# Four row scatters in flight instead of two in the dispatch stage of a two-layer mixture-of-experts kernel

## The reference

```python
x = x + _L0_attn_ref(_layernorm(x), ...)   # 16 heads of 16, causal
x = x + _L0_ffn_ref(_layernorm(x), ...)    # 16 experts, top 2, one shared expert
x = x + _L1_attn_ref(_layernorm(x), ...)   # 16 query heads, one key and value head
x = x + _L1_ffn_ref(_layernorm(x), ...)    # 32 experts, top 8, one shared expert
```

```python
logits = flat @ router_w.T
_, topk_idx = jax.lax.top_k(logits + router_bias, TOPK)
for e in range(N_EXPERTS):
    h = jax.nn.silu(flat @ Wu[e]) * (flat @ Wg[e])
    out = out + combine[:, e:e + 1] * (h @ Wd[e])
for s in range(N_SHARED):
    out = out + jax.nn.silu(flat @ Su[s]) * (flat @ Sg[s]) @ Sd[s]
```

## Time and profile before

| | us |
|---|---|
| median of 3 runs | 1201.76 |
| lowest and highest run | 1192.37, 1206.13 |
| the profiled execution's own time | 1202.92 |
| its span | 1201.1 |

### The profile page before, as it was taken

How to read it: one execution, slowest core, us unless ns; L and a number is a source line. 1 busy time by engine, 2 the same in 40 slices (tenths; PEclk the granted TensorE clock), 3 DMA queues, 4 the chain that set the end, 5 groups by cost and what they waited for, 6 DMA issues and landing times. The chain is left out here.

```text
span 1201.1 us, 22110 instructions
## 1 busy us (share of the span) xinstructions
PE 909.2 (76%) x5927; PEld 701.8 (58%) x5927; DVE 697.1 (58%) x2692; ACT 462.5 (39%) x1172; POOL 624.3 (52%) x878
## 2 busy tenths in 40 slices
PE   2578888888596995179898888628799999999900
PEld 1466666666354883156676655414488887888800
DVE  4778888863532554557677665523245554555568
ACT  2446566653101441247645444200044444444400
POOL 3546565533063554245638888756245655555610
PEclk9858899897688998558969778658899999999955
DMA  8400000000633542300002222229455555555378
GB/s 233 180 2 1 1 1 2 1 2 1 230 110 108 147 137 91 112 1 2 2 1 84 83 94 100 99 100 404 185 164 166 176 174 157 168 152 166 96 300 330
DMA packets 72791, 136.99 MB, mean 114 GB/s; under 512 B 13102, under 2 KB 51421, under 8 KB 70624
## 3 DMA queue, kind: packets, MB, share of 16 engines
q1 hardware_dynamic: 51840, 85.15, 21.9%
q0 software_dynamic: 17632, 46.73, 10.9%
q10 hardware_dynamic: 3200, 3.70, 0.9%
HBM read 79.15 MB, written 62.39 MB: 118 GB/s over the span
## 5 line engine op out<-in xcount | busy, mean ns | idle before, releaser
L2051 POOL DMA_INDIRECT parts<-e_y,e_dest x206 | 202.6, 984 | 186.1 <-issue 98.1
L1946 PE MATMUL e_ps_u<-wres,e_xT 128*128 x824 | 215.4, 384 | 0.1
L1367 POOL TENSOR_SCALAR_AFFINE_SELECT a_probs<-a_probs 128x256 f32<-128x256 f32 x256 | 108.7, 449 | 134.3 <-ACT a_probs L844 133.4
L1946 PEld LDWEIGHTS e_ps_u<-wres,e_xT 128*128 128x128 f32 x824 | 158.0, 193 | 23.4 <-issue 2.0
L1453 POOL DMA_INDIRECT rows<-f_rows,f_place_at x128 | 124.7, 974 | 51.8 <-issue 27.4
L1959 PE MATMUL e_ps_y<-wres,e_hT 128*128 x412 | 124.8, 385 | 8.5 <-ACT e_hT L1992 5.5
L844 ACT ACTIVATE a_probs<-a_ring 128x768 f32<-128x768 f32 x128 | 104.7, 818 | 67.6 <-PE a_ring L611 66.1
L1987 ACT ACTIVATE e_act_out<-e_ps_u 128x128 f32<-128x128 f32 x206 | 57.1, 277 | 180.7 <-issue 95.6
L2016 DVE TENSOR_TENSOR e_hid<-e_act_out,e_ps_u 128x128 f32<-128x128 f32 x206 | 59.3, 288 | 111.1 <-PE e_ps_h L1954 50.2
L1041 DVE CUSTOM_DVE_ANT_0 a_masked<-a_ring,a_ahead 128x128 f32<-128x128 f32 (+1 forms) x256 | 76.0, 352 | 53.9 <-PE a_ring L587 50.8
L2025 DVE TENSOR_SCALAR e_y<-e_ps_y,e_xg 128x256 f32<-128x256 f32 x206 | 99.5, 483 | 1.0 <-issue 1.0
(11 more groups left out here) (300 smaller groups left out, 2036.3 us busy)
## 6 DMA issues: line engine op xcount, KB each, us to landing
e_xg<-rows SPq DMA_DIRECT2D x159, 160.0 KB
wres<-in_experts SPq DMA_DIRECT2D x4, 3072.0 KB
f_rows<-parts SPq DMA_DIRECT2D x8, 1024.0 KB, 7.1
f_xT<-parts SPq DMA_DIRECT2D x8, 1024.0 KB, 7.5
e_xg<-rows SPq DMA_DIRECT2D x47, 144.0 KB
wres<-in_experts SPq DMA_DIRECT2D x4, 1536.0 KB
rows<-empty SPq DMA_DIRECT2D x1, 5120.0 KB, 24.3
e_yk<-parts SPq DMA_DIRECT2D x16, 256.0 KB
```

Of the source, the lines that this page charges most:

```text
L1367: last = nc.gpsimd.affine_select(out=diagonal[:, :, a], in_=diagonal[:, :, a], compare_op=ALU.is_ge, fill=0.0, base=0, pattern=[[0, 2], [1 ...
L1946: last = nc.tensor.matmul(ps_u[b % 2][:, 0:2 * P], xT[b % 2][:, c * P:(c + 1) * P], wres[:, ds(e, 1), 2 * c * P:2 * (c + 1) * P].rearrange ...
L2051: nc.gpsimd.indirect_dma_start(out=parts[:, :], out_offset=bass.IndirectOffsetOnAxis(ap=dest[b % NY][:], axis=0), in_=y[b % NY][:], in_off ...
```

## The change

In `dispatch` the number of semaphores, and with it the number of scatters that may be on their way, becomes IN_FLIGHT = 4 in place of 2. Scatter n waits for scatter n - 4. At the end POOL waits for each of the four semaphores to have its 8 scatters.

```diff
@@ -1524,7 +1524,7 @@
-        scattered = [sem(f"scattered{i}") for i in range(2)]
+        scattered = [sem(f"scattered{i}") for i in range(IN_FLIGHT)]
@@ -1551,12 +1551,12 @@
             for t in range(NT):
                 for k in range(K):
                     n = t * K + k
-                    wait(pool, scattered[n % 2], 16 * (n // 2))
+                    wait(pool, scattered[n % IN_FLIGHT], 16 * (n // IN_FLIGHT))
                     nc.gpsimd.indirect_dma_start(
                         out=rows[:, :], out_offset=bass.IndirectOffsetOnAxis(ap=place_at[:, t, k:k + 1], axis=0),
-                        in_=X[:, t], in_offset=None).then_inc(scattered[n % 2], 16)
-            for i in range(2):
-                pool.wait_ge(scattered[i], 16 * K * NT // 2)
+                        in_=X[:, t], in_offset=None).then_inc(scattered[n % IN_FLIGHT], 16)
+            for i in range(IN_FLIGHT):
+                pool.wait_ge(scattered[i], 16 * K * NT // IN_FLIGHT)
```

## The result

| | before | after |
|---|---|---|
| median | 1198.85 us (4 runs, 1192.37 to 1206.13) | 1220.03 us (4 runs, 1211.65 to 1223.26) |
| profiled execution, span | 1201.1 | 1217.8 |
| ratio after / before | | 1.0195, 95% interval 1.0155 to 1.0235 |

The change makes the kernel about 2% slower; 1198 us had been forecast, with 1192 to 1204 as the range. The same kernel was timed twice more with experiments: 1220.17 us against 1196.73 (ratio 1.0216, interval 1.0150 to 1.0282) and 1219.07 against 1196.63 (1.0179, interval 1.0124 to 1.0235).

What follows compares the result with a forecast made beforehand. `dispatch` was taken as bound by POOL's scatter chain, last at the closing barrier by 3.7 us over PE and DVE's chain. Sum -3.7 + 0 + 0 = -3.7 us: 1201.76 - 3.7 = 1198.1, rounded 1198 us, range 1192 to 1204.

Steps and rivals of the forecast that it cites:

- POOL's pace: Scatters in `dispatch`: without landing waits, starts 1.26 us apart with 0.30 us gaps, the last ending 4.1 us earlier.
- The tail: End of `dispatch`: last scatter's end to the end of POOL's DRAIN stays 4.46 us, so POOL is through at 374.4.
- Rival (a): POOL's DRAIN in `dispatch`: the tail grows to 8.1 us as in attention; saving 0.5, time 1201.3; chance 0.13.
- rival (b): POOL's DRAIN in `dispatch`: work left undone per scatter adds up to 8.0 us owed; slower, 1205.7; chance 0.06.
- Rival (c): Scatters in `dispatch`: landings or POOL already limit the pace, waits only move to n-4; saving 0, 1201.8; chance 0.09.
- (d): PE's clock at the expert stage's start: 1.0 us lost or 2.2 won, 1199.1 or 1195.9; inside the forecast's range.
- DVE reports at 374.8, untouched by the edit: Barrier ending `dispatch`: DVE's report stays at 374.8 and becomes last, so release moves from 378.5; 3.7 us saved.
- The last part of the prediction: List of signs: wrong if PE's or DVE's chain itself ends later, or layer 1 changes by more than the shift.
- The barrier and what follows: After `dispatch`: POOL's barrier instruction right behind DVE's report; clear, second barrier, SP's load (376.8) and PE's start (379.0) move along.
- The rest of the kernel: Expert stage, reduction and layer 1: the shift passes through unchanged, as nothing there waits for a fixed time.

Runs made afterwards that it cites:

- e10: The changed kernel again, unaltered, as control for three further runs; two times, 1199.86 and 1181.77 us, before 1183.94; `dispatch` 65.0 us.
- e16: Against before: 32 extra four-deep scatters of 64-byte rows ahead of the real ones, plus 1200 semaphore increments by SP in attention 0; 1226.35 us against 1185.62.
- e2: The changed kernel's four semaphores, but scatter n waits for scatter n - 2 as before; 1210.48 us against before's 1216.53, ratio 0.9982.
- e4: The changed kernel, but every eighth scatter waits for the one before it; 1213.37 us against before's 1216.53, ratio 0.9980.
- e1: The changed kernel with three semaphores and three scatters in flight instead of four; 1242.18 us against before's 1216.53, ratio 1.0200.
- e3: The changed kernel with one tiny POOL memset behind every scatter; 1230.28 us against before's 1216.53, ratio 1.0102.
- e9: The changed kernel once more, unaltered, as a control; 1220.17 us against before's 1196.73, ratio 1.0216.
- e17: The changed kernel again, unaltered, timed in five rounds; 1219.07 us against before's 1196.63, ratio 1.0179.
- e14: The kernel before, two in flight, plus 600 semaphore increments issued by SP once the slots are ready; 1184.44 us against 1188.92, ratio 0.9982.
- e6: The changed kernel, but scatter 16 alone waits for scatter 15; 1179.79 us against before's 1184.46, ratio 0.9961.
- e8: The changed kernel, but scatter 8 alone waits for scatter 7; 1184.62 us against before's 1184.46, ratio 0.9979.
- e13: The changed kernel, but scatter 16 alone waits for scatter 15, timed again beside a control; 1184.60 us against before's 1183.94, ratio 1.0008.
- e18: Same kernel as e16 (extra thin scatters, SP increments in attention 0), run again in another series; 1254.60 us against before's 1196.63.

## Why the prediction was wrong

**POOL's pace: right.** Forecast were starts 1.26 us apart with gaps of 0.30 us and 40.3 us from the first start to the last end; measured 1.27 us, 0.30 us, and 372.09 + 0.96 - 332.64 = 40.4 us. The landing was as quick as the step assumed: 2.5 us (median of e10). With the 0.30 us gap this gives (2.5 + 0.3) / 2 = 1.40 us for two in flight, the pace of before. The Trainium skill's page "DMA: Bandwidth & Descriptors", section "Anatomy of one DMA", gives an estimate of 2.34 us for these rows and of 2.0 us for the thin ones; e10 has 2.5 us and e16 2.1 for them. The measured times bear the rule out. What the prediction drew from it, that the change would then save nothing, left out the gap.

**The tail: right.** From the end of the last scatter to the end of the DRAIN 377.5 - 373.1 = 4.4 us, forecast 4.46. Rival (a), 8.1 us, and rival (b), an owed backlog, both fall; (b) had the sign of the result, but by POOL's own arrival, which came 22.4 us before the release. Rival (c) falls too, since no scatter waited. So does (d): the half clock ends at 408.8, 4.6 us behind PE's start at 404.20, against 4.4 in before.

**"DVE reports at 374.8, untouched by the edit": the step that failed.** It reported at 399.9. The prediction had priced what the edit does to POOL and to the barrier and took the other chain as given, because no instruction of it was touched and no engine or port was shared that the profile of before showed. The last part of the prediction named this as what would make it wrong, but no case and no chance stood for it. What the runs showed in its place: in the series with late increments those of PE came up to 15 us late at that addition once POOL no longer waited, and DVE reported 25.1 us later. In before POOL's short waits are spread over the whole run (11.3 us in 24 of them): e2, which has them too, and e4, with three breaks, have no stall; after, e1, e3, e9 and e17, where they are gone, have it. Those waits had been booked as pure loss. No row of before priced this, though its trace already has PE increments 0.7 to 3.6 us late in both expert stages and in attention 1, where POOL issues DMAs too; why the increments are late stays open.

**The barrier and what follows: right.** POOL's barrier instructions follow the last report within 0.1 us (399.9, 400.0), and the next stage starts on PE 4.2 us after the release, 404.20 - 400.0, as in before (382.72 - 378.5). A saving of the forecast size is there where nothing is held back: 65.0 us in e10 against 68.2 in e14, so 3.2. In the first series it is in the sum too, hidden: DVE came 25.1 us later, of which 3.7 fill the time that POOL used to be last, and the stage began 1.5 us later (counted from the clearing of the semaphores, L109, at 310.9 and 312.4), so 25.1 - 3.7 - 1.5 = 19.9 us of stage.

**The rest of the kernel: right.** Attention 1, `finish` and experts 1 together +2.6 - 0.4 - 1.9 = +0.3 us. Nothing was forecast for experts 0 either; its -4.9 us goes with the late increments in the trace of before, told above.

No kernel tried here beats both. Those with breaks are within 0.4% of before (e4 in a series with late increments, ratio 0.9980; e6, e8 and e13 in series without, 0.9961, 0.9979 and 1.0008), and the 3 us that the change brings at best is 0.3%, less than these intervals tell apart.

## What to carry to other kernels

A wait on a queue that issues DMAs back to back is not only lost time: before taking it away, look for a chain on other engines that runs beside it, give "that chain is slowed" a case and a price, and keep a break every few issues if the gain is small anyway. When two engines that wait for different things start in the same instant, with "remote" or "issue" as the releaser and the producers long done, look whether the increments were late and not the work. And when an experiment takes an effect away, run the unchanged kernel in the same series before believing it: eleven of the runs here met a series without the effect.

## What the runs showed of the hardware that had not been expected

- While POOL issues indirect DMAs 1.27 us apart without a break, PE's semaphore increments can come 15 us late (362.30 to 377.69 in after) and 20.0 us in e9, and in e18, with 64 scatters, the additions that wait for them stand up to 32 us apart. They come in order, the last ones 60 ns apart. In after, e1, e9 and e17 the last addition that is held back starts 0.1 to 0.4 us behind the end of POOL's 2.67 us DRAIN, in e3 and e18 before that end. Those of DVE and ACT are not held (0.04 us at most).
- It happened in four series of runs of eight, and there with over 40% of the DMA increments missing from the record, most of all in the stage that stalls. In the other four it never happened, and the kernel before was 8 to 33 us faster (1184 to 1189 us against 1197 to 1217). Whether it also happens in executions that are not recorded is not shown.
- POOL's pace doesn't depend on the bytes: 1.27 us between starts for rows of 64 bytes (e18) and of 1152 (e10), with 0.96 us an instruction and 0.30 us between two, and a memset of 0.12 us fits into that gap.
